# Holding the aggregate scatter and the gather by dst on counts of node steps, and letting the first gather run eight groups ahead, in a two-layer graph network

## The reference

```
# layer 0
edge_input = concat(x[src], edge_attr_32)
messages   = gelu(edge_input @ mW1 + mb1) @ mW2 + mb2
gates      = sigmoid(gelu(edge_input @ gW1 + gb1) @ gW2 + gb2)
aggregated = segment_sum(messages * gates, dst)
update     = gelu(concat(x, aggregated) @ uW1 + ub1) @ uW2 + ub2
x1 = layernorm(x + layernorm(x + update) * ln_g + ln_b)
# layer 1
score = exp(clip(sum_heads(K[src] * Q[dst] / sqrt(12) * E), -5, 5))
h     = segment_sum(V[src] * score, dst) / (segment_sum(score, dst) + 1e-6)
out   = layernorm(x1 + h)
```

## Time and profile before

| what | value |
|---|---|
| median of 3 runs | 1746.39 us |
| lowest and highest run | 1743.65 and 1760.29 us |
| the profiled execution's own time | 1731.89 us |
| its span, first to last instruction | 1730.1 us |
| busy: TensorE, VectorE, POOL, ScalarE | 62%, 55%, 54%, 40% of the span |
| mean granted TensorE clock | 0.792 of 2.4 GHz |

### The profile page before, as it was taken

The page is one execution under the profiler, slowest core; times in us unless marked ns, Lnnn a source line. Parts: engine busy times, 40 slices in busy tenths (PEclk is TensorE's granted clock), DMA queues, the critical chain, the costliest instruction groups (busy, mean ns, idle before and its releaser), DMA issues. The chain is left out here.

```text
span 1730.1 us, 20279 instructions
## 1 busy us (share of the span) xinstructions
PE 1080.6 (62%) x5020; PEld 653.0 (38%) x5020; DVE 947.0 (55%) x4244; ACT 692.5 (40%) x1522; POOL 940.2 (54%) x984
## 2 busy tenths in 40 slices
PE   4777878621021199899879992266465765566574
PEld 2333333200010187677768772133232322223231
DVE  3333333200000188889979898176565665566577
ACT  2333334200000048677758787233232333333343
POOL 6565555677777104433433543655566566666555
PEclk9898888755555599989989996587787787887787
DMA  5944443231111036656656663322222222222221
GB/s 115 188 144 125 139 142 107 57 98 39 38 39 48 18 108 203 184 158 198 201 157 177 187 207 120 98 63 58 55 64 59 64 57 67 56 57 67 56 65 37
DMA packets 131958, 178.21 MB, mean 103 GB/s; under 512 B 75125, under 2 KB 76852, under 8 KB 131841
## 3 DMA queue, kind: packets, MB, share of 16 engines
q1 hardware_dynamic: 97741, 130.13, 25.2%
q0 software_dynamic: 31360, 46.18, 10.8%
q10 hardware_dynamic: 2740, 0.60, 0.2%
HBM read 101.31 MB, written 77.56 MB: 103 GB/s over the span
## 5 line engine op out<-in xcount | busy, mean ns | idle before, releaser
L380 POOL DMA_INDIRECT wide<-agg_d,dst_at x196 | 185.9, 949 | 338.7 <-DMA agg_d<-node_work 243.6
L399 POOL DMA_INDIRECT out<-wide,put_at x196 | 192.9, 984 | 145.3 <-ACT wide L701 76.4
L355 POOL DMA_INDIRECT wide<-in_x,src_i x196 | 185.3, 945 | 138.8 <-ACT einT L638 76.3
L392 POOL DMA_INDIRECT node_work<-agg_d,src_i x196 | 188.1, 960 | 103.9 <-issue 58.5
L364 POOL DMA_INDIRECT agg_d<-wide,put_at x196 | 187.9, 959 | 61.2 <-issue 59.7
L559 PE MATMUL ps<-nT,Wks 96*96 96x512 f32 x98 | 75.1, 858 | 206.8 <-ACT nT L711 102.3
L896 DVE BATCH_NORM_STATS2 bn<-ps 128x6 f32<-128x96 f32 x392 | 99.3, 258 | 166.6 <-remote 153.5
L665 ACT ACTIVATE node_work<-node_work,nshift,nscale 128x96 f32<-128x96 f32 x392 | 145.5, 454 | 63.6 <-DVE nshift L933 58.1
L808 DVE SCALAR_TENSOR_TENSOR ps<-hidden,ps 96x512 f32<-96x512 f32 x49 | 33.9, 692 | 249.8 <-ACT hidden L644 196.7
L711 ACT ACTIVATE nT<-ps 96x512 f32<-96x512 f32 x99 | 55.8, 592 | 263.4 <-remote 175.6
L526 PE MATMUL ps<-einT,uW1x 96*96 96x512 f32 x196 | 109.9, 689 | 72.1 <-ACT einT L657 51.6
(11 more groups left out here) (156 smaller groups left out, 2363.3 us busy)
## 6 DMA issues: line engine op xcount, KB each, us to landing
agg_d<-zeros SPq DMA_DIRECT2D x40, 480.0 KB
x_in<-in_x SPq DMA_DIRECT2D x49, 384.0 KB
node_work<-agg_d SPq DMA_DIRECT2D x49, 384.0 KB
agg_d<-node_work SPq DMA_DIRECT2D x49, 384.0 KB
out<-node_work SPq DMA_DIRECT2D x49, 384.0 KB
mask<-cont_d SPq DMA_DIRECT2D x49, 208.0 KB
mask<-cont_d SPq DMA_DIRECT2D x49, 192.0 KB
ea<-in_edge_attr SPq DMA_DIRECT2D x48, 192.0 KB
```

Source lines behind the costliest of these rows:

```text
L355: pool.indirect_dma_start(rows[:, g * EJ + j, :], None, x, rows_at(src_i, g, j)).then_inc(xs_gathered[g % 2], 16)
L380: pool.indirect_dma_start(rows[:, g * EJ + j, :], None, x1_d, rows_at(dst_at, g, j)).then_inc(xd_gathered[g % 3], 16)
L392: pool.indirect_dma_start(ahead[:, g % AHEAD, j, :], None, x1_d, rows_at(src_i, g, j)).then_inc(x1s_gathered[g % 2], 16)
L399: pool.indirect_dma_start(out, rows_at(put_at, g, j), rows[:, g * EJ + j, :], None, bounds_check=N - 1, oob_is_err=False).then_inc(out_sca ...
```

## The change

Four things are changed. The first gather waits for `einT_copied` with a lead of eight groups instead of four. The aggregate scatter of group g, from group 8 on, also waits until `node_summed` has reached `steps_due[g]`, about g/2 - 2 (at least 1), a number that VectorE works out in the prologue and POOL loads into registers four at a time, after the first DMA of each fourth group. `node_summed` is raised once more in the prologue, so that it is never waited for at zero; all other waits on it are shifted by one. And the gather by dst of group g now needs the larger of its old count and g/2 + 20 stored node groups. The attention stage is not touched.

```diff
-LEAD, BEHIND = 4, 7
+EDGE_LEAD, LEAD, BEHIND = 8, 4, 7
+RATE, AFTER, BEFORE = 2, 3, 20
...
                     if i >= 0:
-                        sp.wait_ge(node_summed, i + 1)
+                        sp.wait_ge(node_summed, i + 2)
...
-                if g >= LEAD:
-                    pool.wait_ge(einT_copied, g - LEAD + 1)
+                if g >= EDGE_LEAD:
+                    pool.wait_ge(einT_copied, g - EDGE_LEAD + 1)
...
+            def due_from(g):
+                ahead_of = min(NEEDS, EGROUPS - g)
+                _, values = nc.values_load_multi_w_load_instructions(steps_due[0:1, g:g + ahead_of], engines=[mybir.EngineType.Pool], min_val=1, max_val=NGROUPS + 1)
+                return values
+
             pool.wait_ge(index_made, 2)
             pool.wait_ge(zeros_stored, 16 * ZSTEPS)
+            pool.wait_ge(due_made, 1)
             for g in range(EGROUPS):
                 pool.wait_ge(agg_copied, g + 1)
                 if g >= 2:
                     pool.wait_ge(agg_added[g % 2], of_group(g - 2))
+                if g >= RATE * (AFTER + 1):
+                    pool.wait_ge(node_summed, due[g % NEEDS])
                 for j in range(EJ):
                     pool.indirect_dma_start(agg_d, rows_at(put_at, g, j), rows[:, g * EJ + j, :], None).then_inc(agg_added[g % 2], 16)
+                    if j == 0 and (g + 1) % NEEDS == 0 and RATE * (AFTER + 1) <= g + 1 < EGROUPS:
+                        due = due_from(g + 1)
...
-            pe.matmul(spread_ends, ones[0:1, :], starts_ends[0:1, 0, :], start=True, stop=True)
+            pe.matmul(spread_ends, ones[0:1, :], starts_ends[0:1, 0, :], start=True, stop=True).then_inc(node_summed, 1)
...
                 if i + 1 < NGROUPS:
-                    act.wait_ge(node_summed, i + 2)
+                    act.wait_ge(node_summed, i + 3)
...
             dve.wait_ge(counted, 1)
-            dve.tensor_scalar(pairs[:, 0, :, :], counts, 2.0, 1.0, ALU.max, ALU.add).then_inc(needs_step, 1)
-            dve.tensor_scalar(pairs[:, 1, :, :], counts, 2.0, None, ALU.max).then_inc(needs_step, 1)
+            dve.tensor_scalar(share[:, :], starts_ends[:, 1, :], 1.0 / (RATE * NROWS), None, ALU.mult).then_inc(due_step, 1)
+            dve.tensor_copy(reach[:, 0, :], counts[:, 0, :]).then_inc(due_step, 1)
+            dve.wait_ge(due_step, 2)
+            dve.scalar_tensor_tensor(reach[:, 1, :], share[:, :], float(BEFORE), counts[:, 1, :], ALU.add, ALU.max).then_inc(due_step, 1)
+            dve.memset(steps_due[:, 0:1], 1).then_inc(due_step, 1)
+            dve.tensor_scalar(share[:, :], share[:, :], float(1 - AFTER), 1.0, ALU.add, ALU.max).then_inc(due_step, 1)
+            dve.wait_ge(due_step, 5)
+            dve.scalar_tensor_tensor(share[:, 1:], counts[:, 1, 0:EGROUPS - 1], -1.0, share[:, 1:], ALU.add, ALU.min).then_inc(due_step, 1)
+            dve.wait_ge(due_step, 6)
+            dve.tensor_scalar(steps_due[:, 1:], share[:, 1:], 1.0, None, ALU.max).then_inc(due_made, 1)
+            dve.tensor_scalar(pairs[:, 0, :, :], reach[:, :, :], 2.0, 1.0, ALU.max, ALU.add).then_inc(needs_step, 1)
+            dve.tensor_scalar(pairs[:, 1, :, :], reach[:, :, :], 2.0, None, ALU.max).then_inc(needs_step, 1)
```

More of the change, by code:

```diff
@@ L111, in build @@
         need_agg, need_x1 = need[:, :, 0, :], need[:, :, 1, :]
+        share, reach = sb("share", [1, EGROUPS]), sb("reach", [1, 2, EGROUPS])
+        steps_due = sb("steps_due", [1, EGROUPS], I32)
         put_at = sb("put_at", [P, EGROUPS, EJ], I32)
@@ L180, in build @@
         needs_step, needs_made, spread, counted = sem("needs_step"), sem("needs_made"), sem("spread"), sem("counted")
+        due_step, due_made = sem("due_step"), sem("due_made")
         weights_made, zeros_stored = sem("weights_made"), sem("zeros_stored")
```

## The result

The changed kernel takes **1799.87 us** (median of four runs, 1797.61 to 1802.77) against 1750.33 us for the kernel before, measured beside it (four runs, 1743.65 to 1760.29). The ratio is **1.031 [1.027, 1.035]**: slower, where I had forecast 1682 us. The profiled execution took 1801.55 us with a span of 1799.8.

What follows compares the result with a forecast made beforehand. It took stalls from POOL's unbroken issuing to bound the kernel. Node step 48 coming 65 us earlier turned the profiled 1731.9 us into 1667; 14.5 us up to the median gave 1682 us, range 1615 to 1735.

Steps and rivals of the forecast that it cites:

- Part 3: Node stage beside held scatters, two groups per step: 12.8 us a step, bounds 11.5 and 14, 243 us to step 20.
- Part 4: Node stage with held gathers by dst: 30 us quiet, 230 us at 12.8 a step, 61 at 9.4; step 48 at 982.
- Part 1: Prologue and edge stage, lead of eight: first edge step 20 us later, bounds 0 and 27; steady edge steps stay 6.6 us.
- Part 2: First eight scatter groups, unheld: they end at 359 us, last edge copy at 400, node step 1 at 418, gaining 186 us.
- rival 3: Node stage: TensorE stays at half clock, dense steps take 15.1 us, deciding from 14.6; total 1767 us, 8%.
- The attention: Attention stage: as long as before, 632 us.
- Rival 1: Node stage: register loads break POOL's runs, stalls get short, dense steps take 11.5 us; total 1625 us, 25%.
- Rival 4: Scatters: the hold doesn't hold because counts come out small, POOL scatters without a break as before; total 1750 us, 3%.
- Rival 5: Node stage: VectorE's work blocks POOL's issue through the shared port, dense steps take 18 us; total 1872 us, 3%.
- The rule of 12 us: All engines: POOL issuing over about 12 us without a pause stops the others until about 1.6 us after it pauses.

Runs made afterwards that it cites:

- e4: Kernel before plus a 2.1 us POOL pause after every eight aggregate scatters, no hold, chip 12; ratio 0.949 to the kernel before.
- e5: Kernel before plus a 2.1 us POOL pause after every eight indirect DMAs in all stages, no hold, chip 12; ratio 0.900 to the kernel before.
- e6: Changed kernel, both holds kept, plus a 2.1 us POOL pause after every eight scatters and gathers by dst, chip 12; ratio 0.966 to the kernel before.
- e1: Changed kernel with the first gather's lead back at four groups, both holds kept, chip 12; ratio 1.017 to the kernel before.
- e3: Changed kernel without the hold of the gather by dst, lead eight and scatter hold kept, chip 12; ratio 1.005 to the kernel before.
- e13: The changed kernel measured again as it is, on chip 10; ratio 1.020 to the kernel before.
- e2: Kernel before with only the first gather's lead raised to eight groups, no hold, chip 12; ratio 1.003 to the kernel before.
- e14: Changed kernel with lead four and no hold of the gather by dst, only the scatter hold left, chip 10; ratio 0.999 to the kernel before.
- e9: Changed kernel with lead four and no hold of the gather by dst, only the scatter hold left, chip 7; ratio 0.994 to the kernel before.
- e17: Kernel before plus a 1.2 us POOL pause after every four indirect DMAs in all stages, no hold, chip 3; ratio 0.903 to the kernel before.
- e10: Kernel before plus a 1.2 us POOL pause after every four indirect DMAs in all stages, no hold, chip 7; ratio 1.231 to the kernel before.

## Why the prediction was wrong

That POOL's unbroken issue goes with the stall, and that the holds take away the long hole, was right (e4, e5 and e6 bear the first out), and so were the times up to the first held scatter. The rule for how long a stall lasts wasn't. The step that failed is Part 3, the length of a dense node step, which Part 4 uses again: 12.8 us with bounds of 11.5 and 14, measured 14.9 and 16.3.

- **Part 1, the lead.** First edge step at 56 us forecast, 56.4 measured.
- **Part 2, the first eight groups.** Last gather at 318 forecast, 314.5 + 0.9 measured; the last edge copy at 400 forecast, 393.8 measured; POOL's wait for node step 0 ended at 405.73 (a wait of 49.9 us for L543). Step 1 was 5 us early.
- **Part 3, dense scatter steps.** From step 1 to step 20 the L946 rows took 290 us where I had 243: **+47 us**.
- **Part 4, dense steps of the gather by dst.** The quiet steps to about 745 came as forecast, 8.5 us each. From there to step 48 it took 360 us, where I had 230 + 61: **+69 us**. The dense steps were 16.3 us long, and the 9.4 us steps behind them were fewer.
- These three make -5 + 47 + 69 = 111 us, and step 48's L946 came at 1105.4 where the forecast of 982 for its sum puts it at 994. In break-even terms, both stretches were beyond the 14.6 us from which rival 3 decides.
- **The attention** was forecast unchanged. From its first to its last L1063 it took 599.0 us, 577.5 before, which is the rest of the distance between the profiled executions. I don't count that to the change: with the attention's code the same, that stretch took 575.4 us in e1, 585.6 in e3, 587.5 in e13, 591.6 in e2 (no hold at all), 604.5 in e14.

**Why 12.8 was wrong.** The bound on POOL's own time held: POOL still waited 125.7 us for L543 during the held scatters. I took the value from the attention stage, because it has eight indirect DMAs per step as well. The number of DMAs was the wrong likeness. That a node step has more to catch up with behind a stall (TensorE is busy nearly all of a clean step) is my reading, and no run tests it. What the traces show is that the runs were longer than eight: POOL issued 12 to 16 at a time in most of the first stretch and 15 at a time in most of the second, there with one pause of some 10 us and one of 3.2 to 5.2 between them. A pair of steps took 10.4 + 22.9 = 33 us, 16 more than two clean ones. Some 4 of these are the step at half clock (12.75 for 8.5 us); the other 12 I put down to the stall. e6, whose runs are cut to eight, has 12.7 and 12.9.

**Rival 3** came true in kind: TensorE at half clock behind each stall and runs longer than 12 us in every second step, 15.1 us forecast for 14.9 and 16.3. Its total, 1767 us, was still 33 short, and its runs of twelve and four by rounding are not the 15 and 16 that most of the long ones had. I gave it 8%, and its own argument against (at 12.75 us POOL has 2.5 us of pause in each step) forgot that the pauses come in one piece. **Rival 1** (short stalls) is what e6 came near with real pauses, 12.7 and 12.9 us for its 11.5. **Rival 4** fell: the scatters were held. **Rival 5**, the shared port, fell further: in the node stage of the changed kernel a scatter took 958 ns, and in e9 it took 958 beside a VectorE busy 404 of 416 us. The Trainium skill ("SBUF — State Buffer", two separate sides) says that a two-port VectorE operation locks GpSimd out; these rows show no such delay, and no run tests whether this kernel's VectorE has operations of that kind.

**What I could have seen.** The rule of 12 us came from stalls in the edge stage and the prologue. In the node stage of the changed kernel ScalarE is late sooner: its inputs were complete at 836.40, 3.9 us into POOL's run of 832.52, and it started 6.1 us after that. The forecast asked it to hold for a stage with another mix, and took the price of a stall there from a third stage. Bounds from two stages that don't contain the operation in question should have been wider than 11.5 to 14: the break-even of 14.6 stood just outside them, so the sign hung on half a microsecond per step. And the trace of before spoke against a fixed end of the stall: its scatters end at 573.6, and the others start at 596.5.

## What to carry to other kernels

Where one engine's unbroken issue stalls the others, spreading its work by waits on the others' progress made lumps here, runs of up to 16 DMAs; pauses on the issuing engine itself, 2.1 us after every eight or 1.2 after every four, took 10% off where the holds cost 2 to 3%. When work is moved beside a full stage, find the step length at which the gain is gone before choosing a value, and if it lies within a few tenths of your bounds, give the other sign its share. And measure on more than one chip: the pauses of e17 gain 10% on chip 3, and the same kernel loses 23% on chip 7, where there was no stall (e10).

## What the runs showed of the hardware

- Unbroken indirect DMAs on POOL, 1.27 us apart, slow TensorE to one transpose each 2.80 us and hold up ScalarE and VectorE with it. What is contended no run shows. The Trainium skill ("Runtime: NRT & Kernel Launch", instruction fetch mechanics) says that instruction fetch is hidden behind issue; nothing here tests whether that still holds in the stall.
- The effect isn't there in every set of runs: the same kernel takes 1262 us on chip 7 and 1728 to 1756 us on chips 3, 10 and 12, and a gather or scatter takes POOL the same on all of them (medians of 944 to 963 ns). Chip 12 was used twice and had it twice, with 1728 and 1751 us; chip 7 once.
- On chips 3, 10 and 12 a POOL pause of 2.1 us after eight DMAs, kept up from the start, keeps the long stall away, and so does 1.2 us after four (0.900, 0.899, 0.903 of the time); 1.2 after eight and 2.1 after sixteen don't. The others stay stopped the longer the run was: 1.6 to 3.0 us behind 12 to 16 DMAs, 4.0 and 6.1 behind 36 and 37, 22.9 behind 196.
- POOL needs 0.94 to 0.98 us (medians) and a gap of 0.30 us for an indirect DMA of 128 rows, in the stall and out of it. A load of eight register values takes 3.2 to 3.6 us in most cases, up to 5.2.
